# A graph attention layer on one core: source rows as float32r pairs, three of four heads added by TensorE, and no GpSimd arithmetic beside the sort

## What is computed

```python
def head(w1, bb1, w2, bb2, a1, aab1, a2, aab2):
    feats = jnp.maximum(x @ w1 + bb1, 0.0) @ w2 + bb2             # (n, 64)
    x_cat = jnp.concatenate([feats[row], feats[col], elem[:, None]], axis=1)
    hid = jnp.maximum(x_cat @ a1 + aab1, 0.0)                     # (edges, 129)
    e1 = (hid @ a2 + aab2)[:, 0]
    e1 = jax.nn.leaky_relu(e1, negative_slope=0.2)
    w = jnp.exp(e1 - jnp.max(e1))
    pooled = jax.ops.segment_sum(w[:, None] * feats[col], row, num_segments=n)
    row_sum = jax.ops.segment_sum(w, row, num_segments=n) + 1e-10
    return pooled / row_sum[:, None]
x = _layernorm(x + heads_side_by_side)
```

## Time and profile before

| | us |
|---|---|
| median of 3 runs | 4868.68 (4866.79 to 4869.52) |
| span of the profiled execution, first to last instruction | 4828.3 |
| what lies around the span, median less span | 40.4 |
| busy: PE, DVE, ACT, POOL | 4260.4, 4460.2, 3835.5, 2693.5 |
| start; sort and tables; records; main loop; end | 165; 1335; 60; 3150; 118 |

### The profile page before, as it was taken

The page is one execution under the profiler, slowest core; times in us unless marked ns, Lnnn a source line. Parts: engine busy times, 40 slices in busy tenths (PEclk is TensorE's granted clock), DMA queues, the critical chain, the costliest instruction groups (busy, mean ns, idle before and its releaser), DMA issues.

```text
span 4828.3 us, 133194 instructions
## 1 busy us (share of the span) xinstructions
PE 4260.4 (88%) x24114; PEld 3004.1 (62%) x24115; DVE 4460.2 (92%) x25378; ACT 3835.5 (79%) x12983; POOL 2693.5 (56%) x2886
## 2 busy tenths in 40 slices
PE   1598998898896999999999999999999999999990
PEld 1355555555555777777777777777777777777760
DVE  8799999999996999999999999999999999999998
ACT  1587778778774888888888888888888888888884
POOL 5366666666664555555555555555555555555544
PEclk9999999999997999999999999999999999999995
DMA  2133333333334877777777777777777777777757
GB/s 85 43 73 86 79 71 80 81 77 80 79 76 137 240 225 221 228 225 224 224 225 224 225 225 221 226 224 224 225 224 224 224 225 225 225 225 225 221 172 212
DMA packets 266918, 851.82 MB, mean 176 GB/s; under 512 B 107916, under 2 KB 109584, under 8 KB 266861
## 3 DMA queue, kind: packets, MB, share of 16 engines
q0 software_dynamic: 169920, 673.54, 50.0%
q1 hardware_dynamic: 63543, 160.18, 11.2%
q10 hardware_dynamic: 33398, 17.49, 1.4%
HBM read 739.10 MB, written 111.90 MB: 176 GB/s over the span
## 4 chain that ended last, share of the span: by engine, by line
PE 36%; ACT 27%; issue 3%; DVE 2%; DMA 1%; ACTq 0%; POOL 0%; DVEq 0%; SPq 0%; POOLq 0%
ACT z L1164 18%; PE psum L971 15%; PE psum L975 9%; PE psum L958 8%; ACT onehot L1193 3%; ACT onehot_t L1182 3%; PE psum L984 3%; ACT onehot L1197 2%; PE psum L939 1%; DVE z L1689 1%; DVE z L1682 0%; PE psum L995 0%; ACT onehot L1195 0%; DVE z L1705 0%; DMA p_win<-p_table 0%
## 5 line engine op out<-in xcount | busy, mean ns | idle before, releaser
L754 POOL DMA_INDIRECT z<-qf_table,rec x1664 | 1609.2, 967 | 1454.9 <-PE psum L958 1027.1
L1164 ACT ACTIVATE z<-z 128x64 f32<-128x64 f32 x6656 | 1651.1, 335 | 0.0
L971 PE MATMUL psum<-p_win,onehot_t 128*128 x9984 | 1407.8, 274 | 84.1 <-ACT onehot_t L1182 68.3
L971 PEld LDWEIGHTS psum<-p_win,onehot_t 128*128 128x128 bf16 x9984 | 966.8, 97 | 540.0 <-issue 214.4
L958 PE MATMUL psum<-z,onehot 128*128 128x260 f32 x3328 | 1029.4, 391 | 6.7 <-DVE acc L1617 4.9
L975 PE MATMUL psum<-z,ident 128*128 128x258 f32 x3328 | 1002.7, 383 | 0.0
L1568 DVE SCALAR_TENSOR_TENSOR z<-z,a_b 128x129 f32<-128x129 f32 x3328 | 884.3, 290 | 5.6 <-issue 0.2
L1568 DVE SCALAR_TENSOR_TENSOR z<-psum,a_b 128x129 f32<-128x129 f32 x3328 | 828.2, 286 | 0.0
L1558 DVE TENSOR_TENSOR z<-z,psum 128x258 f32<-128x258 f32 x1664 | 698.6, 420 | 94.6 <-PE psum L975 90.6
L1617 DVE TENSOR_TENSOR acc<-acc,psum 125x260 f32 x1664 | 702.3, 422 | 25.3 <-PE psum L958 2.4
L695 POOL DMA_INDIRECT sorted_rows<-z x300 | 478.5, 1595 | 403.9 <-DVE z L1447 321.6
(11 more groups left out here) (220 smaller groups left out, 5576.3 us busy)
## 6 DMA issues: line engine op xcount, KB each, us to landing
p_table<-acc SPq DMA_DIRECT2D x100, 338.6 KB
p_win<-p_table SPq DMA_DIRECT2D x100, 338.6 KB
z<-qf_table,rec POOLq DMA_INDIRECT x1664, 4.5
qf_table<-acc SPq DMA_DIRECT2D x75, 339.5 KB
acc<-in_x_dram SPq DMA_DIRECT2D x25, 448.0 KB
z<-in_x_dram SPq DMA_DIRECT2D x20, 560.0 KB
out_dram<-z ACTq DMA_DIRECT2D x20, 560.0 KB
qf_table<-z SPq DMA_DIRECT2D x25, 339.5 KB
```

The lines of the kernel that those rows point to most:

```text
L754: pool.indirect_dma_start(out=z_t[:, o + j, :], out_offset=None, in_=qf_table, in_offset=bass.IndirectOffsetOnAxis(ap=rec[:, o + j, 3:4].b ...
L971: mm = pe.matmul(to, onehot_t[:, j, :], p_flat[:, bass.ds((w % 2) * (3 * ZW) + (part * ZW + o), n)], start=(part == 0), stop=(part == 2 an ...
L1164: op = act.activation(z_t[:, slot, o:o + DO], z_t[:, slot, o:o + DO], ACT.Copy, scale=z_t[:, slot, o + DO:o + HF])
```

## The change

- `p_table` and `p_win` hold two float32r parts (value rounded, and rest) and not three bf16 parts: 4,128 bytes a row and not 3,096. `onehot_t` is float32r.
- PEH = 3: PE adds Q for heads 1 to 3. Bank one holds columns 0 to 129 (130 columns), bank two columns 128 to 515 (388 columns). A tile has two float32r matmuls of 130 columns, two of 388, and a float32 matmul of 388 columns by the identity. DVE adds Q for head 0 alone (129 columns), and takes three scores from PSUM and one from `z`.
- `split_p` and `p_sum` go. The bias comes in by two bf16 matmuls with three rows ahead of each `p_product`. ACT copies and rounds PSUM to the first part (`take_p`), DVE subtracts (`p_rest`) and writes the second; PE waits on `s_p_lo` where it waited on `s_p_ev`.
- POOL splits the bias row into three bf16 parts at the start (five operations on one partition), ahead of the first mask; SP waits for these ahead of the fills of `sorted_rows`, and moves them with three transfers.
- `win_pack` and `end_prev` move into a free row of `acc`: made in `z`, carried over by one transfer of SP after ACT's last clearing and before the first records are loaded.
- Constants and scratch tiles of the sort move into `z` and `acc`; `iota_win` has one row of 100 and not four.

```diff
-    PEH = 2
-    NA = (H - PEH) * AT if PEH else HALF
-    NB = ZW - NA
+    PEH = 3
+    NV = (H - PEH) * AT
+    NO = NV + 1
+    TO = NV - 1
@@ SP
+            sp.wait_ge(s_ab_step, 5)
+            for u in range(3):
+                sp.dma_start(ab1_rows[u:u + 1, :], ab1_parts[0:1, u * ZW:(u + 1) * ZW]).then_inc(s_ab_rows, 16)
             sp.wait_ge(s_empty, 1)
...
             sp.wait_ge(s_tab_step, N_TAB_STEPS)
+            sp.wait_ge(s_acc_zero, 1 + BULK)
+            sp.dma_start(tables, made).then_inc(s_tab_st, 16)
+            sp.wait_ge(s_tab_st, 16)
@@ POOL
+            br, rest, bp = ab1_row[0:1, :], ab1_rest[0:1, :], ab1_parts[0:1, :].rearrange("p (u n) -> p u n", u=3)
+            pool.tensor_copy(bp[:, 0, :], br).then_inc(s_ab_step, 1)
...
-            order = [(split_p, -1, 3), (scatter, 0, 0), (scatter, 0, 1), (scatter, 0, 2), (split_p, 0, 0), (split_p, 0, 1),
-                     (scatter, 0, 3), (split_p, 0, 2)]
@@ PE
-                since(pe, s_p_ev, n)
+                since(pe, s_p_lo, n)
                 for q in range(2):
-                    mm = pe.matmul(psum[0:WN, 5 + q, 0:HALF], f_t[:, q, at], ad_p[:, q, :], start=True, stop=True)
+                    pe.matmul(psum[0:WN, 5 + q, 0:HALF], ones_b[0:3, 0:WN], ab1_rows[0:3, q * HALF:(q + 1) * HALF], start=True, stop=False)
+                for q in range(2):
+                    mm = pe.matmul(psum[0:WN, 5 + q, 0:HALF], f_t[:, q, at], ad_p[:, q, :], start=False, stop=True)
...
-                    for o, n, to in ((0, NA, z_one(slot)), (NA, NB, z_two(slot))):
-                        for part in range(3):
+                    for o, n, to in ((0, NO, z_one(slot)), (TO, ZW - TO, z_two(slot))):
+                        for part in range(2):
...
+                    mm = pe.matmul(z_two(slot), ident[:, :], z_t[:, slot, TO:ZW], start=False, stop=True, skip_group_check=True)
@@ ACT
+            def take_p(g, w):
+                n = g * 4 + w
+                act.wait_ge(s_p_mm, n + 1)
+                since(act, s_p_st[w % 2], g * 64 + w // 2 * 32)
+                act.activation(p_out[0:WN, w % 2, 0:ZW].bitcast(F32R).rearrange("p (q n) -> p q n", q=2), psum[0:WN, 5:7, 0:HALF], ACT.Copy).then_inc(s_p_hi, 1)
@@ DVE
+            def p_rest(g, w):
+                dve.wait_ge(s_p_hi, g * 4 + w + 1)
+                dve.tensor_tensor(p_out[0:WN, w % 2, ZW:2 * ZW].bitcast(F32R).rearrange("p (q n) -> p q n", q=2), psum[0:WN, 5:7, 0:HALF],
+                                  p_out[0:WN, w % 2, 0:ZW].rearrange("p (q n) -> p q n", q=2), ALU.subtract).then_inc(s_p_lo, 1)
-            beside = {11: [(0, p_sum, 0)], 13: [(0, p_sum, 1)], 15: [(0, p_sum, 2)], 1: [(-1, p_sum, 3)]}
+            beside = {12: [(0, p_rest, 0)], 14: [(0, p_rest, 1)], 0: [(-1, p_rest, 2)], 2: [(-1, p_rest, 3)]}
...
+                    own = z_t[:, slot, 0:NV]
+                    dve.tensor_tensor(own, own, z_one(slot)[:, 0:NV], ALU.add).then_inc(s_z_added, 1)
```

More of the change, by code:

```diff
@@ L27 @@
 BF16 = mybir.dt.bfloat16
+F32R = mybir.dt.float32r
 AX_X = mybir.AxisListType.X
@@ L217, in gnn_layer @@
         before_f = carve_z(P)
+        ones_b = carve_z(P // 2).bitcast(BF16)
+        before = carve_z(P // 2).bitcast(BF16)
+        iota_win = carve_z(W // 2).bitcast(BF16)
         counts = carve_z(W)
@@ L637, in _ @@
                                fill=1.0, base=0, channel_multiplier=1).then_inc(s_const, 1)
-            pool.affine_select(out=before[:, :], in_=ones_b[:, :], pattern=[[1, P]], compare_op=ALU.is_ge,
+            pool.affine_select(out=before, in_=ones_b, pattern=[[1, P]], compare_op=ALU.is_ge,
                                fill=0.0, base=-1, channel_multiplier=-1).then_inc(s_const, 1)
@@ L643, in _ @@
             pool.tensor_copy(ident_b, ident[:, :]).then_inc(s_const, 1)
[L644 removed]
+            pool.tensor_copy(before_f, before).then_inc(s_const, 1)
             pool.affine_select(out=same_col, in_=ones_f[:, 0:HCOL * LO].rearrange("p (c n) -> p c n", c=HCOL), pattern=[[-HI, HCOL], [0, LO]],
@@ L697, in scatter @@
                         in_=rows_out[0:KB[k], (b - 3) % 2, 2 * (W + 1) + k * SF:2 * (W + 1) + (k + 1) * SF], in_offset=None, compute_op=ALU.add).then_inc(s_scat, 16)
-            def split_p(g, w):
-                n, b = g * 4 + w, w % 2
-                pf = p_f[0:WN, b, :]
-                pool.wait_ge(s_p_ev, n + 1)
-                since(pool, s_p_st[b], g * 64 + w // 2 * 32)
-                pool.sem_inc(s_passed, 1)
-                pool.tensor_copy(p_out[0:WN, b, 0:ZW], pf).then_inc(s_p_hi, 1)
-                pool.wait_ge(s_p_hi, n + 1)
-                pool.tensor_tensor(pf, pf, p_out[0:WN, b, 0:ZW], ALU.subtract).then_inc(s_p_rest, 1)
-                pool.wait_ge(s_p_rest, n + 1)
-                pool.sem_inc(s_passed, 1)
-                pool.tensor_copy(p_out[0:WN, b, ZW:2 * ZW], pf).then_inc(s_p_mid, 1)
-                pool.wait_ge(s_p_mid, n + 1)
-                pool.tensor_tensor(p_out[0:WN, b, 2 * ZW:3 * ZW], pf, p_out[0:WN, b, ZW:2 * ZW], ALU.subtract).then_inc(s_p_lo, 1)
-            order = [(split_p, -1, 3), (scatter, 0, 0), (scatter, 0, 1), (scatter, 0, 2), (split_p, 0, 0), (split_p, 0, 1),
-                     (scatter, 0, 3), (split_p, 0, 2)]
             def group(g):
-                for work, off, n in order:
-                    if work is scatter and isinstance(g, int) and g * PER + n - 3 == BLOCKS - 1:
+                for n in range(PER):
+                    if isinstance(g, int) and g * PER + n - 3 == BLOCKS - 1:
                         pool.wait_ge(s_sum, 4 * BLOCKS)
                         pool.iota(win_iota, [[P, NT]], base=0, channel_multiplier=0, allow_small_or_imprecise_dtypes=True).then_inc(s_win_iota, 1)
-                    if (live_b(g, n, -3) if work is scatter else not isinstance(g, int) or 0 <= g + off < GROUPS):
-                        work(g + off, n)
+                    if live_b(g, n, -3):
+                        scatter(g, n)
             sort_loop(pool, group)
@@ L863, in feats @@
                 if m == 0:
-                    since(pe, s_p_ev, g * 4)
+                    since(pe, s_p_lo, g * 4)
                 pe.wait_ge(s_h_ev, g * MC + m + 1)
@@ L968, in hidden_src @@
                     pe.wait_ge(s_win_ready, w + 1)
[L969 to L975 removed]
+                    for o, n, to in ((0, NO, z_one(slot)), (TO, ZW - TO, z_two(slot))):
+                        for part in range(2):
+                            pe.matmul(to, onehot_t[:, j, :], p_flat[:, bass.ds((w % 2) * (2 * ZW) + (part * ZW + o), n)],
+                                      start=(part == 0), stop=(part == 1 and o == 0), skip_group_check=True)
+                    pe.wait_ge(s_gather[slot], i * 16 + 16)
+                    mm = pe.matmul(z_two(slot), ident[:, :], z_t[:, slot, TO:ZW], start=False, stop=True, skip_group_check=True)
                     mm.then_inc(s_z_mm, 1)
@@ L1121, in group @@
                         take_rows(g, b)
-                    for work, *args in beside.get(q, []):
-                        if not isinstance(g, int) or g < GROUPS:
-                            work(g, *args)
+                    for off, work, *args in beside.get(q, []):
+                        if not isinstance(g, int) or 0 <= g + off < GROUPS:
+                            work(g + off, *args)
             act.dma_start(base_rows_d[:, :, :].rearrange("h u n -> h (u n)"), base_hl[0:BLOCKS, :].bitcast(BF16)).then_inc(s_base_st, 16)
@@ L1573, in own_dot @@
                     if h == 0:
-                        dve.wait_ge(s_z_added if PEH else s_z_free, tile(0, j) + 1)
+                        dve.wait_ge(s_z_added, tile(0, j) + 1)
                     op = dot(slot, h, z_t[:, slot, h * AT:(h + 1) * AT])
```

142 lines of the change are left out of this document (68 added, 74 removed).

## The result

The changed kernel takes 5008.52 us (5008.13 to 5010.24, four runs) beside 4869.1 (4866.79 to 4870.23) for the kernel before: a ratio of 1.029, 95% interval 1.027 to 1.030. It is 139 us slower where 32 us less were forecast. Its profiled execution took 5008.51 us with a span of 5006.3. A second profile of the kernel before (`before_again`) took 4871.43 us with a span of 4869.7: some 2 us lie around a span. The 40.4 us of the prediction are therefore not something around the span: the profiled execution of the earlier trace rows, whose own time is not on record, must have been a short one of some 4830 us, 38 of the 41 us in the main loop (3134.9 us from first to last selection against 3173.1). From here on the stretches are compared with `before_again`.

The account below looks back on a forecast made before the run. It took DVE as fullest in the sort and a ring of ACT and PE as holding the main loop; -112 (sort) + 5 (start) + 75 (loop) = -32 us gave 4837 us, range 4750 to 5110.

Parts of the forecast that it names:

- Step (5): Sort: PE's next product waits for ACT's copy, then DVE's subtraction; up to 1 us after products 2 and 3.
- Rival E: Sort gives nothing, because PE, waiting for the copy and the subtraction, holds it; 4949 us, chance 0.08.
- Step (1): Sort: without `split_p` on POOL, DVE's one-hots and row-number operations get shorter, 181 us, or 7.2 us of a group.
- Step (4): Sort: two bf16 matmuls of 258 columns a product on PE, 0.22 us each product, 0.9 us a group.
- Step (3): Sort: ACT gets a copy of 516 columns, 0.589 us, 100 times; 2.4 us a group.
- Steps (2), (6) and (10): `p_rest` of `p_sum`'s size, P stores a third larger, window loads 129 KB more, ACT's four-byte copy: each costs nothing.
- Start and step into the loop: POOL's five operations ahead of the first mask, and the table transfer before the first record load: +5 us (0 to 8).
- Step (9): Main loop: float32r selection on PE, 0.11 us a narrow matmul, 0.166 a wide one; 0.55 us, 0.11 less than before.
- Step (8): Main loop: PE's identity matmul has 388 columns and not 258, +0.215 us a tile.
- ring: Main loop super-block: about 10.4 us of ACT and waiting, then 4.7 us of PE with three tiles' source selections.
- Step (7): Main loop: DVE adds 129 columns and not 258, 224 us of DVE in all, worth nothing.
- Rivals A, B, C and D: Main loop: A narrow matmul 0.056 us, 4762, 0.13; B 0.22, 5089, 0.28; C half float32 price, 5250, 0.05; D float32, 6700, 0.04.

Follow-up runs that it names:

- rest_first: The changed kernel with `p_rest` moved behind the picks and ahead of the slot one-hots in DVE's step; 4887.32 us, ratio 1.002 to the kernel before.
- quiet_pool: The kernel before with the four POOL operations of `split_p` cut to 4 columns of 516; 4751.9 us, ratio 0.975.
- add_129: The kernel before with DVE adding Q and P for 129 columns of a tile and not 258; 4873.07 us, ratio 0.9994.
- narrow_to_256: The changed kernel with the two matmuls to the first bank 256 columns wide and not 130; 5014.13 us, ratio 1.030 to the kernel before.
- dve_frees_and_adds: The changed kernel with DVE copying P from PSUM and adding the bias, ACT rounding from SBUF, no bias matmuls; 4951.76 us, ratio 1.016 to the kernel before.
- round_later: `dve_frees_and_adds` with ACT's rounding and DVE's subtraction one step later in their orders; 4864.52 us, ratio 0.997 to the kernel before.

## Why the prediction was wrong, step by step

- **Step (5), the waits, failed.** It charged PE nothing after products 0 and 1 and up to 1 us after products 2 and 3, because the subtraction stands "one step q later". It looked at the right places: nearly all of the wait lies after product 2. It had its length wrong, because it never asked what stands in DVE's step ahead of the subtraction. The one of product 2 falls in step 0, which opens a block: there the slot one-hots and a set of chunk one-hots stood ahead of it for 3.3 us, and PE stood 3.5 us in each group. (The one of product 0, in step 12, stands behind slot one-hots too, and PE hardly waits for it.) With `p_rest` ahead of them the sort is 121 us shorter (`rest_first`), 4.8 us a group. The clock in the sort was not in the forecast either: 43 of the 121 us are PE's own work at a lower clock behind the waits. Rival E named this mechanism, but at a chance of 0.08, and charged it only the forecast gain; it took 47 us more than that.
- **The base of the sum was also off.** The group of 53.40 us was taken for the mean; from first to last one-hot it is (1490.8 - 185.6) / 25 = 52.2 us. The group summed to was 48.9, `rest_first` has 49.1 in the timeline and (1419.8 - 188.8) / 25 = 49.2 as a mean. So steps (1) to (4), with 1.5 us put on top for waits, gave the right group, but the gain from it is 3.0 us and not 4.5: about 74 us for the sort, not 112. With these 74 and no other step changed the forecast would have been +6 against before, no gain; `rest_first`, without the wait, measured 1.002. So step (5) is 121 of the 139 us by which the kernel is slower, but the gain that was forecast would not have come without it either.
- **Step (1), contention: right.** One-hots at a mean of 303 ns, worth 124 us by itself (`quiet_pool`), with PE as the cap; DVE lost 167 us of busy time for the 181 summed. **Step (4), the bias matmuls: right**, 20 us for 22. **Step (3), the copy on ACT:** 59.6 us of busy time for 100, as forecast; what it cost in waits was not tried by itself.
- **Steps (2), (6) and (10): right.** `p_rest` takes 0.68 us; no store of P stands among the long waits of the sort, and the window loads are at 0% of the chain.
- **Start and step into the loop:** +3.2 and +0.4 for 4 and 1.
- **The main loop: right in its prices, near in size.** Step (9): the narrow matmul 0.11 us, as forecast, the wide 0.177 for 0.166, the selection 0.57 for 0.55. Step (8): 0.65 us. Per tile 1.66 - 1.54 = +0.12 for +0.105, and +86 us for +75. The forecast had ring and PE about equally full; measured, PE alone holds the loop. By its starts PE has 24 x 1.66 + 3.9 = 43.7 us of work in a body that takes 3259.3 / 69.3 = 47.0; what the other 3.3 us are was not told apart. Step (7), DVE's lighter addition worth nothing: shown by `add_129` for the kernel before, and its 224 us of DVE were 141. Rivals A, B, C and D fall with the timeline and `narrow_to_256`.
- **Around the span:** the 40.4 us were the difference between one short execution and the median of others. They cancelled in the sum, which was made against the median by way of them.

The forecast of 4837 us missed by 171.5: 121 by the order in DVE's step, 38 by the size of the sort's gain (112 less 74), 11 in the loop, less 1 at the start, and 3 because the second profile of before stands 3 us above the median the forecast started from.

## What to carry to other kernels

When a wait on a semaphore moves to another instruction, read off what stands ahead of that instruction in its engine's order at just those steps, and what stands behind the waiting one; an operation that frees a resource for the fullest engine belongs first in its step. A repair that only moves the wait to a third in-order engine gives back what it gained (`dve_frees_and_adds`); moving the consumer by one step in that engine's order brought 91 us (`round_later`). And a high busy share is no promise: DVE was busy for 93% of the loop and at 2% of the chain, and work taken off it bought nothing (`add_129`), while the third head's addition, put on PE, which was in the chain, helped to make PE the whole of it. The reverse holds too: POOL was at 0% of the chain, and its arithmetic still cost 124 us, by making DVE's instructions longer (`quiet_pool`). Ask what an operation does to its neighbours before calling it free.

## What the runs showed of the hardware

- A float32r matmul takes nearly the bf16 time per column: 388 columns in 0.177 us (0.325 + 0.325 for float32), 258 in 0.12 where bf16 has 0.11. But weights of 128 float32r columns take 190 ns to load and not 97, and within the selection (L985) two such loads never start less than 0.109 us apart, in 4992 pairs. So the 130-column matmul costs 0.11 us and not the 0.06 that its columns ask for: 126 more columns (`narrow_to_256`) add 3.4 ns a tile. The change's split of 130 and 388 pays this for half of its matmuls, equal banks do not: 0.57 us a tile against 0.48.
- One idle gap of 3.5 us on PE is followed by over 4 us at a granted clock of 0.50. In the sort of the changed kernel such stretches were worth 43 of the 121 us that the waits cost. The Trainium skill ("TensorE: Matmul & The Clock Gate", Part 1) names two levels, of which the engine has the lower one after being idle; the rows above agree.
- The Trainium skill ("SBUF — State Buffer", Who interferes with whom) has GpSimd and VectorE, in its two-port modes or with two SBUF inputs, take turns at a shared port pair. The trace agrees in direction, and `quiet_pool` puts a number on it: operations of 516 columns on POOL, cut to 4, return 133 us of the one-hots' busy time (1600 x (388 - 305) ns) and 124 us of the sort. Which mode DVE's instructions ran in no run shows.
